# Edge stage of a four-layer graph network: four tiles summed in one cleared PSUM bank, one 512-column add on VectorE

## The chip, the cores and the metric

The kernel runs on one core of one Trainium2 chip, as one launch. The metric is the device time of a launch in microseconds: before the change three timed runs gave 4739.2, 4741.78 and 4747.91, median 4741.78 us. Beside them stands one profiled execution of the same kernel.

## The reference, cut to what matters

Four graph layers follow one another on 6250 nodes of 128 features; the edge list has 106250 entries (50000 drawn edges in both directions and a loop at every node), sorted by `dst`. Only the last layer is touched:

```
e_in     = concat([x[src], x[dst]])                    # per edge
edge_new = relu(e_in @ We1 + be1) @ We2 + be2
agg      = segment_sum(edge_new, dst, num_segments=N)
mesh_new = relu(concat([x, agg]) @ Wn1 + bn1) @ Wn2 + bn2
x        = layernorm(x + (x + mesh_new))
```

The first product splits in two node products, P = x·We1(upper) and Q = x·We1(lower) + be1, so an edge needs relu(P[src] + Q[dst]), and We2 can be applied after the sum over edges. The edge stage computes, for each node, the sum of relu(P[src] + Q[dst]) over its edges.

## The kernel before, in words

**Tiles.** Nodes lie in 49 blocks of 128. Edges are put in an order of the kernel's own and cut into 960 tiles of 128 edges, so that all edges of a tile have their `dst` in one block. Three sections follow one another: edges that need only the first 3 of 13 groups of P rows and have `dst` in blocks 0 to 29; the rest of those that need the first 6; and all others. In each the blocks rise. Within the setup stage VectorE works out each edge's sort value (lines 2569 to 2610), POOL scatters them to their places (line 1741), and VectorE writes the block number of every tile into the SBUF row `block_of` (lines 2700 to 2703).

**Spots.** The edge stage takes 8 tiles at a time: 120 spots, `Spot` in the code. The first 96 are 16 turns of six (`TURN = "DEDEDE"`); turn 0 and turn 15 are written out, turns 1 to 14 run in hardware loops; the last 24 are written out too. Of an "E" spot the rows P[src] were gathered earlier and come in by one DMA, of a "D" spot POOL gathers them now, eight indirect DMAs of 128 rows (line 1134). 48 spots are E, 72 are D, and the last 24 are all D.

**One spot**, on four engines that each run their own list in order:

- ACT turns the tile's `dst` values into a one-hot matrix with edges along the free side (lines 1206, 1208), then applies Relu to the two halves (line 1223).
- PE loads 8 block numbers from `block_of` into registers (`tile_blocks`, line 471; `snap`, line 472), multiplies the turned one-hots with Q of those blocks (line 1253, "q" below, fp32, 4 tiles in each of two banks), and then sums the spot before: one fp32 product per tile, relu'd rows times one-hot, 128 columns of its own in PSUM (line 1234, "sums" below). A second half of q waits for VectorE's first half of the spot before (semaphore `edge_pre`).
- VectorE makes the other one-hots for the next spot (line 1268, "hots"), loads the spot before's 8 block numbers, adds P rows and q of this spot in two halves of 512 columns (line 1284), and then adds the eight PSUM results of the spot before to `acc` at their blocks, one instruction of 128 columns per tile (line 1294), each waiting for the one ahead of it.
- SP issues the broadcasts of `dst` values and the E rows.

In PE's list q waits for `hot_ready`, which VectorE gives one spot earlier. In turns 0 to 12 PE also does half of a node product (lines 1240, 1241), which ACT copies (line 1218) before PE goes on.

Of the kernel before, what the change touches and what calls it, by code (L numbers as in the profile page):

```python
# [12 lines left out]
BF16 = mybir.dt.bfloat16  # L13
I32 = mybir.dt.int32
# [20 lines left out]
VB = NEAR_BLOCKS + 2 * NB  # L35
T = -(-((E + VB * (P - 1)) // P) // (2 * CH)) * 2 * CH
# [118 lines left out]
def gnn(nc, d):  # L155
    ctx = ExitStack()
    with ctx:
# [48 lines left out]
        ext_w = sb("ext_w", [P, EXT_BLOCKS])  # L206
        mv = sb("mv", [P, NBP, 2])
# [249 lines left out]
        hid_added = Count(S("added"), T)  # L457
# [9 lines left out]
        def tile_blocks(eng, c, which="block"):  # L467

            if (eng, which) not in block_regs:
                block_regs[eng, which] = [eng.alloc_register(f"{which}{u}") for u in range(CH)]  # L470
            eng.load(block_regs[eng, which], block_of[0:1, bass.ds(CH * c, CH)])  # L471
            return [eng.snap(r, min_val=0, max_val=NB - 1) for r in block_regs[eng, which]]  # L472
# [753 lines left out]
        def edge_pe(pe):  # L1226

            def sums_of(spot):
                h = spot.par
                for g, tiles in groups(P):  # L1230
                    wait(pe, S("added"), CH * (spot.u - 2) + tiles[-1] + 1)
                    wait(pe, S("edge_act"), 2 * spot.u + g + 1)
                    for u in tiles:
                        nc.tensor.matmul(psum_sum(h, u, P), ring_e[:, h * CH + u, :], hot_ring[spot.hot][:, u, :],  # L1234
                                         start=True, stop=True, skip_group_check=True).then_inc(S("summed"), 1)
# [7 lines left out]
            def body(spot):  # L1243
# [5 lines left out]
                wait(pe, S("hot_ready"), spot.u + 1)  # L1249
# [15 lines left out]
        def edge_dve(dve):  # L1265
# [8 lines left out]
            chain(dve)(nc.vector.tensor_copy(iota_bank, iota[:, :]))  # L1274
            hots(Spot(0, 0))
            chain(dve)(nc.vector.memset(acc[:, :], 0.0))
            last_of = {u: tiles[-1] for g, tiles in groups(P) for u in tiles}
# [10 lines left out]
            def adds_of(spot, blk):  # L1288
                for u in range(CH):
                    if u == 0 or last_of[u] != last_of[u - 1]:  # L1290
                        wait(dve, S("summed"), CH * spot.u + last_of[u] + 1)
                    dst = acc[:, bass.ds(blk[u] * P, P)]
                    wait(dve, S("added"), CH * spot.u + u)
                    nc.vector.tensor_tensor(dst, psum_sum(spot.par, u, P), dst, ALU.add).then_inc(S("added"), 1)  # L1294

            def body(spot):
                if not spot.last:
                    hots(spot.after())
                if not spot.first:
                    blk = tile_blocks(dve, spot.before().chunk)  # L1300
                gathered(spot)
                if not spot.first:
                    adds_of(spot.before(), blk)
                if spot.last:
                    adds_of(spot, tile_blocks(dve, spot.chunk))
# [1002 lines left out]
        def _(dve):  # L2308
# [261 lines left out]
            near_left, far_before, from_far = tiny[:, 10:11], first, edge_b[4][:, 0:EC]  # L2570
            step(nc.vector.tensor_scalar(behind_near, src_s, float(NEAR_TO), None, ALU.is_ge))
            step(nc.vector.scalar_tensor_tensor(behind_near, dst_s, float(NEAR_BLOCKS * P), behind_near, ALU.is_ge, ALU.max))
# [21 lines left out]
            step(nc.vector.scalar_tensor_tensor(key_i, behind_near, float(NEAR_BLOCKS * P), dst_s, ALU.mult, ALU.add))  # L2594
            step(nc.vector.scalar_tensor_tensor(key_i, far, float(NB * P), key_i, ALU.mult, ALU.add))
# [3 lines left out]
            step(nc.vector.tensor_copy(near_left, extra_ends[:, 0:1]))  # L2599
            counted_before(far_before, far)  # L2600
            step(nc.vector.scalar_tensor_tensor(prod, place, 2.0, ee, ALU.mult, ALU.subtract))
# [366 lines left out]
```

## Time and profile before

| what | value |
|---|---|
| median of three timed runs | 4741.78 us (4739.2 to 4747.91) |
| the profiled execution's span, first to last instruction | 7303.0 us |
| mean granted TensorE clock in it | 0.754 |
| busy over the span: PE, VectorE, ACT, POOL | 56%, 46%, 32%, 36% |
| edge stage in the profiled execution | about 6205 to 7255 us |

The profiled execution gives its span alone, no time of what lies around it, and this span is 2561 us longer than the timed median. It is therefore read for durations and order inside a stage, and not for shares of the timed run. The edge stage's own rows are to be read by spot: one line 1268 instruction on VectorE marks one spot.

### The profile page before, as it was taken

What the parts mean: (1) busy time and instruction counts of PE and PEld (TensorE: products, weight loads), DVE (VectorE), ACT (ScalarE), POOL (GpSimd) and SP (SyncE); (2) the same over time, 40 slices, a digit from 0 to 9 for tenths busy, and PEclk for the clock granted to TensorE, in tenths of its full rate; (3) what the DMA queues carried; (4) which work ended last, traced back from release to release, by engine and by line L of the source; (5) the groups of instructions that cost most, each with busy time, mean ns of one, the idle gap of its engine ahead of it and who ended that gap; (6) DMA issues with size and microseconds to landing.
All of it is one profiled execution on the core that took longest, in us unless ns stands there. A gap on an engine that the chain in (4) does not pass through costs nothing. (4 is left out here: it accounts for less than half of the span.)

```text
span 7303.0 us, 82736 instructions
## 1 busy us (share of the span) xinstructions
PE 4076.2 (56%) x24237; PEld 3354.5 (46%) x24238; DVE 3381.7 (46%) x7886; ACT 2340.3 (32%) x3120; POOL 2658.9 (36%) x2706
## 2 busy tenths in 40 slices
PE   4332641019981111117989798988672197666655
PEld 2111420007761101106778586858571197665644
DVE  4222540358970000106788776456451076555545
ACT  0000010005640000004555455557461075444433
POOL 4555157730017777770000000000427601444463
PEclk7665865559995555558999898989785598888777
DMA  9400000009970000116658287843444343444432
GB/s 376 155 0 0 0 2 0 0 23 334 368 250 0 0 0 0 28 25 222 232 189 293 96 293 214 296 162 95 132 125 124 97 139 98 132 132 130 130 95 67
DMA packets 364823, 923.20 MB, mean 126 GB/s; under 512 B 114026, under 2 KB 138716, under 8 KB 364531
## 3 DMA queue, kind: packets, MB, share of 16 engines
q1 hardware_dynamic: 214722, 650.09, 26.9%
q10 hardware_dynamic: 58609, 180.13, 6.4%
q0 software_dynamic: 91200, 89.42, 5.2%
q8 instruction: 142, 2.33, 0.1%
q14 instruction: 150, 1.23, 0.0%
HBM read 705.69 MB, written 213.71 MB: 126 GB/s over the span
## 5 line engine op out<-in xcount | busy, mean ns | idle before, releaser
L1741 POOL DMA_INDIRECT edges_halves<-local,gather_idx x832 | 854.9, 1027 | 791.7 <-SPq L372 505.4
L1680 POOL DMA_INDIRECT adj_t<-cell_val,cell_at x832 | 828.6, 996 | 465.2 <-issue 369.9
L862 PE MATMUL ps<-tiles_r,stage_r 128*128 128x512 f32 x2028 | 811.6, 400 | 158.2 <-issue 132.0
L1134 POOL DMA_INDIRECT big<-table,gather_idx x576 | 548.4, 952 | 832.3 <-DVE stage L1284 376.3
L869 PE MATMUL ps<-stage,big 128*128 128x130 f32 x4046 | 520.1, 284 | 370.3 <-issue 354.7
L1134 POOL DMA_INDIRECT x_fm<-table,gather_idx x384 | 370.2, 964 | 959.8 <-DMA table<-cell_at 689.7
L869 PEld LDWEIGHTS ps<-stage,big 128*128 128x128 f32 x4046 | 497.9, 199 | 388.5 <-issue 384.6
L2059 PE MATMUL ps<-big,ident_h 128*128 128x104 bf16 (+1 forms) x2880 | 359.7, 256 | 460.4 <-issue 459.7
L1253 PE MATMUL ps<-big,stage 128*128 x1920 | 356.2, 342 | 352.7 <-issue 189.3
L1319 PE MATMUL ps<-ident,big 128*128 128x128 f32 x260 | 73.3, 377 | 817.2 <-issue 768.2
L2442 DVE TENSOR_TENSOR big<-ps,stage 128x1248 bf16<-128x1248 f32 x192 | 270.7, 1451 | 519.5 <-remote 385.1
L755 ACT ACTIVATE big<-big,cols,stage 128x512 f32 (+1 forms) x508 | 371.7, 803 | 428.1 <-remote 273.9
L862 PEld LDWEIGHTS ps<-tiles_r,stage_r 128*128 128x128 f32 x2028 | 389.0, 192 | 257.3 <-issue 154.9
L2059 PEld LDWEIGHTS ps<-big,ident_h 128*128 128x128 bf16 x2880 | 233.9, 103 | 587.8 <-issue 515.3
L1253 PEld LDWEIGHTS ps<-big,stage 128*128 128x128 f32 x1920 | 307.2, 242 | 401.5 <-issue 401.2
L702 DVE TENSOR_SCALAR_CACHE_REDUCE big<-ps 128x512 f16<-128x512 f16 (+2 forms) x724 | 430.0, 651 | 131.4 <-remote 77.9
L797 ACT CAST tiles_r<-onehot 128x1024 fp32r<-128x1024 f16 x338 | 355.0, 1050 | 380.4 <-DMA onehot<-adj_t 127.1
L1746 POOL DMA_INDIRECT big<-edges_halves,pair_idx x8 | 7.7, 958 | 1196.5 <-DVEq L372 1194.4
L1319 PEld LDWEIGHTS ps<-ident,big 128*128 128x128 f32 x260 | 37.1, 181 | 854.7 <-issue 803.8
L864 PE MATMUL ps<-tiles_r,lower_r 128*128 128x512 f32 x1016 | 405.9, 400 | 0.0
L864 PE MATMUL ps<-tiles_r,lower_late 128*128 128x512 f32 x1012 | 398.8, 394 | 0.0
L2761 DVE SCALAR_TENSOR_TENSOR big<-ps,cols,big 128x256 f32<-128x256 f32 x78 | 37.4, 480 | 720.1 <-remote 658.3
(482 smaller groups left out, 9007.8 us busy)
## 6 DMA issues: line engine op xcount, KB each, us to landing
onehot<-adj_t SPq DMA_DIRECT2D x332, 512.0 KB
big<-adj_t SPq DMA_DIRECT2D x332, 512.0 KB
onehot<-adj_s SPq DMA_DIRECT2D x170, 512.0 KB
adj_t<-rows ACTq DMA_DIRECT2D x13, 6656.0 KB
adj_s<-big ACTq DMA_DIRECT2D x157, 512.0 KB, 5.3
stage<-local_rows SPq DMA_DIRECT2D x120, 512.0 KB
big<-adj_s SPq DMA_DIRECT2D x84, 512.0 KB
x_fm<-adj_s SPq DMA_DIRECT2D x84, 512.0 KB
```

What stands on the lines that cost most here:

```text
L702: last = nc.vector.tensor_scalar(turned[turn % RING][:, j, of, :].rearrange("p m c -> p (m c)"), flips[turn % 2][:, j, of, :].rearrange("p ...
L755: nc.scalar.activation(tile32[s][:, m * GW:(m + 1) * GW], r_rows[:, bass.ds(g * GW, GW)], ACT.Relu, bias=col(MINUS_ONE), scale=stage_nm[:, ...
L797: nc.scalar.copy(tile_r[s][:, 0:TW // 2], raw_tile(p, s)[:, 0:TW // 2]).then_inc(S("cast_act"), 1)
L862: nc.tensor.matmul(psum_fm(p, n)[:, 0:cut], upper_rows[:, k, :], tile[:, 0:cut], start=k == 0, stop=False, skip_group_check=True)
L864: last = nc.tensor.matmul(psum_fm(p, n)[:, 0:cut], lower_of(p)[:, k, :], tile[:, 0:cut], start=False, stop=k == NBP - 1, skip_group_check= ...
L869: last = nc.tensor.matmul(psum_nm(p, n, j), tile[:, j * P:(j + 1) * P], stage_nm[:, k, 0:AW], start=k == 0 and j % 2 == 0, stop=k == NBP - ...
L1134: return nc.gpsimd.indirect_dma_start(out, None, table[0:N, :], bass.IndirectOffsetOnAxis(gather_idx[:, t:t + 1], 0))
L1253: last = nc.tensor.matmul(spot.q_bank(g)[:, (u % 4) * P:(u % 4 + 1) * P], ring_ohT[:, h * CH + u, :], q_nm[:, bass.ds(blk[u] * P, P)], sta ...
L1680: nc.gpsimd.indirect_dma_start(out, bass.IndirectOffsetOnAxis(cells[:, c:c + 1], 0), cell_val[:, c:c + 1], None).then_inc(S(name), 16)
L1741: nc.gpsimd.indirect_dma_start(edges_halves, bass.IndirectOffsetOnAxis(slot_at[:, at:at + 1], 0), slot_val[:, at:at + 1], None).then_inc(h ...
L2059: return nc.tensor.matmul(ps[:, bank, of], stationary, moving, start=False, stop=True, skip_group_check=True)
L2442: nc.vector.tensor_tensor(eq[done % 4], own_keys(n).unsqueeze(1).to_broadcast([P, SHIFTS, SLW]), bass.AP(behind.tensor, behind.offset, [be ...
```

## The change

A window of four neighbouring tiles now has one cleared PSUM bank of 512 columns, which stands for four neighbouring blocks. PE clears it with a bf16 product of `ident_h` and a blank operand, and then adds each tile's product (`start=False`) at the 128 columns of its block within the window. VectorE adds the whole bank to `acc` in one 512-column instruction, so two adds for a spot in place of eight. For this the tiles' order must let any four neighbours span at most four blocks: the first section now takes blocks 19 to 48 rising, the middle one runs backward from 48 to 0, the last one rises again. Three tables replace the one: the block of a tile, its column within the window, the window's first block. PE loads a second set of 8 registers per spot, VectorE loads 2 in place of 8.

```diff
@@ sums_of (PE), lines 1228 on
-                for g, tiles in groups(P):
-                    wait(pe, S("added"), CH * (spot.u - 2) + tiles[-1] + 1)
+                column = tile_columns(pe, spot.chunk)
+                wait(pe, S("hot_ready"), spot.u + 1)
+                for g in range(2):
+                    wait(pe, S("added"), 2 * (spot.u - 2) + g + 1)
+                    nc.tensor.matmul(ps[:, 2 * h + g, :], ident_h[:, :], blank, start=True, stop=True,
+                                     skip_group_check=True)
                     wait(pe, S("edge_act"), 2 * spot.u + g + 1)
-                    for u in tiles:
-                        nc.tensor.matmul(psum_sum(h, u, P), ring_e[:, h * CH + u, :], hot_ring[spot.hot][:, u, :],
-                                         start=True, stop=True, skip_group_check=True).then_inc(S("summed"), 1)
+                    for u in range(WINDOW * g, WINDOW * (g + 1)):
+                        last = nc.tensor.matmul(ps[:, 2 * h + g, bass.ds(column[u] * P, P)], ring_e[:, h * CH + u, :],
+                                                hot_ring[spot.hot][:, u, :], start=False, stop=True, skip_group_check=True)
+                    last.then_inc(S("summed"), 1)
@@ body (PE): q no longer waits for the hots
                 wait(pe, S("hot_turned"), spot.u + 1)
-                wait(pe, S("hot_ready"), spot.u + 1)
@@ VectorE
-            def adds_of(spot, blk):
-                for u in range(CH):
...
-                    nc.vector.tensor_tensor(dst, psum_sum(spot.par, u, P), dst, ALU.add).then_inc(S("added"), 1)
+            def add_of(spot, g, window):
+                wait(dve, S("summed"), 2 * spot.u + g + 1)
+                wait(dve, S("added"), 2 * spot.u + g)
+                dst = acc[:, bass.ds(window[g] * P, WINDOW * P)]
+                nc.vector.tensor_tensor(dst, ps[:, 2 * spot.par + g, :], dst, ALU.add).then_inc(S("added"), 1)
             def body(spot):
+                if not spot.first:
+                    window = half_windows(dve, spot.before().chunk)
+                gathered(spot)
+                if not spot.first:
+                    add_of(spot.before(), 0, window)
                 if not spot.last:
                     hots(spot.after())
                 if not spot.first:
-                    blk = tile_blocks(dve, spot.before().chunk)
-                gathered(spot)
-                if not spot.first:
-                    adds_of(spot.before(), blk)
+                    add_of(spot.before(), 1, window)
@@ setup: sort value of an edge (832 columns each)
+            step(nc.vector.tensor_scalar(backward, dst_s, 7, 8, ALU.logical_shift_right, ALU.logical_shift_left))
+            step(nc.vector.tensor_tensor(middle, behind_near, far, ALU.subtract))
+            step(nc.vector.tensor_tensor(backward, backward, middle, ALU.mult))
...
@@ setup: tables, twice, 480 columns each; the four steps of 2700 to 2703 become ten
+                step(nc.vector.tensor_scalar(later_half, block, -2.0, float(NEAR_BLOCKS + NB - 1 - NEAR_FROM), ALU.mult, ALU.add))
...
+                step(nc.vector.tensor_reduce(windows, later_half.rearrange("p (w t) -> p w t", t=WINDOW), AX_X, ALU.min))
...
```

`tile_columns` and `half_windows` are `tile_blocks` with another table and with 8 and 2 values. The blank operand is `w_hh` read as bf16, set to zero once ahead of the stage.

## Rows read from the trace of the kernel before

**Rows 1.** The page: chain that ended last; two groups of indirect DMAs.

```profile
PE 13%; issue 10%; DVE 4%; DVEq 3%; another core or an unknown queue 2%; ACT 0%; DMA 0%; SPq 0%; ACTq 0%
...
L1741 POOL DMA_INDIRECT edges_halves<-local,gather_idx x832 | 854.9, 1027 | 791.7 <-SPq L372 505.4
...
L1134 POOL DMA_INDIRECT big<-table,gather_idx x576 | 548.4, 952 | 832.3 <-DVE stage L1284 376.3
```

**Rows 2.** Busy us (instructions) by engine, PEclk, DMA: looped part, last spots.

```profile
6250.00:6983.00 733.00, 496.04 (x2994) 446.57 (x2993) 430.75 (x1008) 319.57 (x379) 348.58 (x367) 0.82 0.42 130
6983.00:7255.00 272.00, 128.95 (x697) 114.97 (x695) 104.22 (x248) 72.31 (x86) 153.94 (x162) 0.68 0.28 77
```

**Rows 3.** Line 1268 in 6250 to 6980 us: count and ns min/median/max.

```profile
L1268 DVE TENSOR_TENSOR onehot<-ps,local x61: 1211/1212/1225, 6249.0 to 6971.6; 128x1024 f32<-128x1024 f32 x61
L1268 DVE TENSOR_TENSOR rows<-ps,local x31: 1211/1211/1225, 6256.0 to 6978.1; 128x1024 f32<-128x1024 f32 x31
```

**Rows 4.** Timeline of VectorE, one looped spot: start, duration, instruction, count, idle before it.

```profile
6509.02 1.21 DVE L1268 TENSOR_TENSOR onehot<-ps,local 128x1024 f32<-128x1024 f32 x1
6511.37 1.29 DVE L1284 TENSOR_TENSOR stage<-ps,big 128x512 f32<-128x512 f32 x2 [1.14 <-issue]
...
6514.38 1.59 DVE L1294 TENSOR_TENSOR acc<-ps,acc 128x128 f32 x4 [0.21 <-DVE acc L1294]
6515.89 1.21 DVE L1268 TENSOR_TENSOR onehot<-ps,local 128x1024 f32<-128x1024 f32 x1
```

**Rows 5.** Timeline of VectorE, one written-out spot.

```profile
6965.08 1.21 DVE L1268 TENSOR_TENSOR onehot<-ps,local 128x1024 f32<-128x1024 f32 x1
...
6971.60 1.21 DVE L1268 TENSOR_TENSOR onehot<-ps,local 128x1024 f32<-128x1024 f32 x1
```

**Rows 6.** Register loads by line, ns min/median/max: 8, 8 values, snap, 1 value.

```profile
L471 PEldq TENSOR_LOAD <-block_of x120: 1917/1922/1942, 6196.5 to 7235.5; - x120
L471 DVEq TENSOR_LOAD <-block_of x120: 686/1827/1850, 6211.2 to 7251.9; - x120
...
L472 PEldq FUSED_REGOPS  x120: 150/172/176, 6198.5 to 7237.4; - x120
...
L583 SPq TENSOR_LOAD <-need x13: 262/271/813, 1567.3 to 2092.5; - x13
```

**Rows 7.** Timeline of PE: a spot that waits for nobody, then a pause.

```profile
6546.02 2.05 PE L1253 MATMUL ps<-big,stage 128*128 x16 [0.47 <-issue]
6547.90 1.95 PE L1234 MATMUL ps<-onehot,stage 128*128 128x128 f32 x16
6550.36 1.93 PE L1253 MATMUL ps<-big,stage 128*128 x14 [0.51 <-issue]
6553.36 0.27 PE L1253 MATMUL ps<-big,stage 128*128 x1 [1.07 <-issue]
```

**Rows 8.** Timeline of PE: q at the lower clock; q that waited for hots.

```profile
6561.41 3.78 PE L1253 MATMUL ps<-big,stage 128*128 x16 [2.22 <-DVE onehot L1268]
...
6575.23 1.15 PE L1253 MATMUL ps<-big,stage 128*128 x8 [2.30 <-DVE rows L1268]
```

**Rows 9.** PE's address steps ahead of four q products, in 6569.8 to 6570.3 us.

```profile
L1253 PEldq FUSED_REGOPS  x4: 46/46/46, 6569.9 to 6570.3; - x4
```

**Rows 10.** Waits, 6250 to 6983: who, for whom, us, times, longest.

```profile
ACT x_fm L1218 <- remote: 60.2, 8, 9.2
```

**Rows 11.** Waits in 6983 to 7255 us.

```profile
DVE stage L1284 <- remote: 77.4, 11, 10.7
```

**Rows 12.** 512-column add; 416-column bf16 product. Columns as in rows 3.

```profile
L1284 DVE TENSOR_TENSOR stage<-ps,big x240: 678/691/693, 6209.5 to 7248.2; 128x512 f32<-128x512 f32 x120
...
L2055 PE MATMUL ps<-rows,ident_h x16: 339/526/534, 31.2 to 910.6; 128*128 128x416 bf16 x8, 128*128 128x392 bf16 x8
```

**Rows 13.** Setup steps on VectorE: a 480-column one and an 832-column one.

```profile
L2703 DVE TENSOR_TENSOR block_of<-big 128x480 int16<-128x480 f32 x2 | 1.3, 658 | 0.1
...
L2604 DVE SCALAR_TENSOR_TENSOR big<-big,acc x1: 1085/1085/1085, 984.4 to 984.4; 128x832 f32<-128x832 f32 x1
```

More of the change, by code:

```diff
@@ L206, in gnn @@
         ext_w = sb("ext_w", [P, EXT_BLOCKS])
+        block_row, column_row, window_row = block_of[0:32, :], block_of[32:64, :], block_of[64:96, 0:T // WINDOW]
+        blank = w_hh.bitcast(BF16)[:, 0:WINDOW * P]
         mv = sb("mv", [P, NBP, 2])
@@ L465, in gnn, with values_at, tile_blocks, tile_columns @@
         block_regs = {}
-        def tile_blocks(eng, c, which="block"):
+        def values_at(eng, which, table, per, c, most):
             if (eng, which) not in block_regs:
-                block_regs[eng, which] = [eng.alloc_register(f"{which}{u}") for u in range(CH)]
-            eng.load(block_regs[eng, which], block_of[0:1, bass.ds(CH * c, CH)])
-            return [eng.snap(r, min_val=0, max_val=NB - 1) for r in block_regs[eng, which]]
+                block_regs[eng, which] = [eng.alloc_register(f"{which}{u}") for u in range(per)]
+            eng.load(block_regs[eng, which], table[0:1, bass.ds(per * c, per)])
+            return [eng.snap(r, min_val=0, max_val=most) for r in block_regs[eng, which]]
+        def tile_blocks(eng, c):
+            return values_at(eng, "block", block_row, CH, c, NB - 1)
+        def tile_columns(eng, c):
+            return values_at(eng, "column", column_row, CH, c, WINDOW - 1)
+        def half_windows(eng, c):
+            return values_at(eng, "window", window_row, CH // WINDOW, c, NB - 1)
         def groups(w):
@@ L1274, in edge_dve @@
             chain(dve)(nc.vector.tensor_copy(iota_bank, iota[:, :]))
+            chain(dve)(nc.vector.memset(blank, 0.0))
             hots(Spot(0, 0))
             chain(dve)(nc.vector.memset(acc[:, :], 0.0))
-            last_of = {u: tiles[-1] for g, tiles in groups(P) for u in tiles}
             def gathered(spot):
@@ L2569, in _ @@
             behind_near, far, key_i = edge_a[0][:, 0:EC], col_v.bitcast(F32), ahead.bitcast(I32)
[L2570 removed]
+            far_before, from_far = first, edge_b[4][:, 0:EC]
+            middle, backward = edge_b[4][:, 0:EC], edge_b[5][:, 0:EC].bitcast(I32)
             step(nc.vector.tensor_scalar(behind_near, src_s, float(NEAR_TO), None, ALU.is_ge))
[L2572 removed]
+            step(nc.vector.scalar_tensor_tensor(behind_near, dst_s, float(NEAR_FROM * P), behind_near, ALU.is_lt, ALU.max))
             step(nc.vector.tensor_scalar(far, src_s, float(MIDDLE_TO), None, ALU.is_ge))
```

49 lines of the change are left out of this document (28 added, 21 removed).

## The prediction

> **What bounds the kernel now.** I read the page first. Its chain of waits attributes little of the span, and the profiled span is 7303.0 us where the timed median is 4741.78. The two differ by 2561 us. The page's groups show where that can lie: POOL's indirect DMAs, some 2640 of them, each busy 0.95 to 1.03 us [rows 1]; if nearly all of that were the profiler's, 2640 times 0.97 is 2561. That is an argument and not a measurement, but it says that a stage in which POOL is late in the profile need not be so in a timed run. So I take durations from the profile and add my sum to the timed median.
>
> Next, the edge stage by stretches. In the looped part, 733 us hold 61 + 31 = 92 spots [rows 2, 3], 7.97 us each, and no engine is full: PE 496 us, VectorE 431, ACT 320, POOL 349. The timeline shows the limit all the same. One undisturbed spot on VectorE runs from 6509.02 to 6515.89 us, 6.87 us, without a pause that another engine causes: hots 1.21, then 1.14 of "issue", the two 512-column adds 1.29, then eight block adds of which four take 1.59, with 0.21 between the fours [rows 4]. The 1.14 is VectorE's own register load: 8 values take 1.83 us [rows 6], it starts with the hots, and what is longer than they are is left over. So VectorE's own list sets the best spot. Written out, without counters to compute, a spot takes 6.52 us [rows 5]. The other 7.97 - 6.87 = 1.10 us per spot are disturbances: PE pauses such as 1.07 us ahead of a single product [rows 7], and ACT's wait of 60.2 us in all for the node product, eight times [rows 10].
>
> PE is second. When nobody held it up, one spot took 6550.36 - 6546.02 = 4.34 us, at the clock's upper level [rows 7]. Elsewhere q had to wait 2.2 to 2.3 us and started when the hots were there [rows 8]. POOL waits for VectorE in the stage, 376.3 us of it [rows 1]; only in the last 24 spots, all gathers, is it late in the profile: VectorE waits 77.4 us for "remote", which is the landing of rows [rows 11], and 272 us go into some 24 spots [rows 2].
>
> **The change, part by part.**
>
> *VectorE, per spot.* Eight adds go (1.59 + 0.21 + 1.59 = 3.39 us), two 512-column adds come; their price is that of the add of the same shape, 0.69 us each [rows 12]. The load falls from 8 values to 2 and now stands ahead of everything, beside the last add of the spot before. For 2 values there is no row; one value takes 0.27 us on SP, eight 1.83 [rows 6]. I take 0.5, close to the one-value row, and charge nothing: 0.69 us of add cover it. New list: 1.29 + 0.69 + 1.21 + 0.69 = 3.9, with semaphore steps 4.0 us in place of 6.87. If VectorE stayed the bound, 2.9 us per spot would be gained.
>
> *PE, per spot.* This is where I expect the price. PE's instruction list gets a second load of 8 values, 1.92 us, and its snap, 0.17 [rows 6], with address and start steps some 2.25 us. Can it hide? The first load does: it is issued when the sums are all queued, and q starts 0.51 us after the sums' end although the load is 1.92 long [rows 7]. But what stands behind a load isn't issued before it is done; VectorE's 1.14 us show it [rows 4]. The second load stands between q and the sums. It covers q's execution, the first covers the sums', but both stand in one list, and the list's length is then the spot. 4.34 us, which was mostly that list already (load 1.92, snap 0.17, address steps and waits), becomes 6.6.
>
> The eight sums now need an address step each, because their column is a register: q's four steps begin within 0.4 us, 0.13 apart [rows 9], so eight are 1.0 us at most, and nothing if they run beside what issuing a product takes anyway. I take the middle, 0.5. Two blanks and one more wait: a 416-column bf16 product takes 0.53 us at the low clock, 0.34 at best [rows 12]; where the list is the bound it is only the issue that counts. Bounds 0.15 and 1.1; I take 0.25, because PE's array has slack at the upper clock (4 of 7.4 us busy). PE's spot is then 4.34 + 2.25 + 0.5 + 0.25 = 7.35, call it 7.4 us; with all low ends 6.75, with all high ends 8.7.
>
> *What is late next.* PE's 7.4 is above VectorE's old 6.87. q no longer waits for the hots, which takes away the old link, but PE's own list takes its place. Behind PE's second load stand the sums, VectorE's adds of that spot and q of the next. ACT (two 1.1 us steps, two 0.6 us steps) and SP (broadcast, early rows) have slack of over 3 us. VectorE will have 3 us of idle time per spot. POOL's gathers are released by VectorE's 512-column adds, and come with them.
>
> *Sum.* 7.4 - 6.87 = 0.53 us per spot. I keep the disturbances at 1.10 us, so a looped spot goes from 7.97 to 8.50: 92 spots, +49 us. For the 28 written-out spots I take the same 0.53, 6.52 to 7.05: +15. In the profiled execution 24 of these hide behind POOL, so the profiled span grows less.
>
> *Setup.* The sort value costs two more 832-column steps, 1.09 us each [rows 13], less three one-column steps: +1.7. The tables cost ten steps in place of four, twice: twelve more at up to 0.66 us [rows 13], some on a quarter of the columns or on 32 rows, taken at 0.6: +7. They end the stage and the next begins behind them, so all of it is on the path: +9 in all (bounds 4 and 12). The blank's memset is below 0.3 us. The order of the edges changes which rows are gathered when, not how many; nothing counted.
>
> Total: +49 + 15 + 9 = +73, 4741.8 + 73 = 4815 us. For the profiled span: 0.53 times 96 plus 9, 7303 + 60 = 7363.
>
> **The rivals.**
>
> *VectorE's gain arrives (faster).* If PE's second load lay beside q as cheaply as the first lies beside the sums, PE's spot would be 4.34 + 0.5 + 0.25 = 5.1, above VectorE's 4.0: -1.77 us times 120, plus 9, gives 4741.8 - 203 = 4538 us. For it: VectorE bounds the best spots today, and half of its list goes. Against it: PE has 6.87 - 4.34 = 2.5 us to spare per spot and is asked for 3.0. The point from which it decides is PE's added list at 2.5 us. The Trainium skill's page VectorE: DVE Perf Modes, in its section on the TRN2 errata, says that operations on SBUF data pay a fixed cost per instruction, and advises tiles of 512 elements or more. By that rule alone this change pays, and it would come out near this rival; the trace agrees on the add itself (four of 128 columns 1.59 us, one of 512 0.69).
>
> *The disturbances are soaked up (slightly faster).* Today's 1.10 us are partly VectorE's own pauses and waits of VectorE for PE. A PE that runs 7.4 us at every spot, with VectorE idle 3, may show fewer. At 7.4 flat: 92 times -0.57, plus 15 and 9, is -28: 4714 us. Against it: the pauses and the node wait seen above are PE's, and PE will have no slack for them.
>
> *PE at the low clock (slower than forecast).* The granted clock is 0.82 in the looped part [rows 2], so PE is at 1.2 GHz for part of it; 16 q products then take 3.78 us where they took 2.05 [rows 7, 8]. At that level q, sums and two blanks are 3.41 + 3.41 + 1.06 = 7.9 us per spot (3.41 is 3.78 less the last product's own tail), and the array is the bound: 0.5 more per spot, +60, 4875 us. The new pause between q and sums speaks for it. The Trainium skill's page TensorE: Matmul & The Clock Gate, section on HAM oscillation, says that pauses between bursts of products bring the slow level back; a load between q and sums is such a pause.
>
> *It doesn't do what it says.* If lists on both engines end within 0.1 us of today's (the sums' address steps free and the blanks too: 4.34 + 2.25 + 0.15 = 6.74), the stage stays where it is and the setup's 9 us alone are left, partly paid back: 4745 us.
>
> **How the numbers follow.** Forecast 4815: 0.46. Low clock, 4875: 0.20. VectorE's gain, 4538: 0.14. Disturbances soaked up, 4714: 0.14. Nothing, 4745: 0.06. The likeliest case's own range, from PE's spot at 6.75 to 8.2 us (8.7 would need every high end at once), is 4736 to 4910. The range given, 4700 to 4890, leaves out the gain of VectorE and the end of the low-clock case, some 0.2. A change of under 0.2% (9.5 us) can't be told from none; faster by more: 0.14 + 0.13 = 0.27; within: 0.09 (the nothing case and the forecast's low edge); slower: 0.64.
>
> **What would show it.** Right: a spot of PE at 7.2 to 7.6 us with two register loads of 1.9 us in it; VectorE idle about 3 us per spot, waiting for PE's products; adds at 0.69; the looped part about 780 us. VectorE's step: its list at 4.0. Sums' address steps: their spacing against q's. Low clock: a granted clock under 0.75 there and products spaced 0.21. Setup: the table steps 12 more. Wrong: spots of 5 to 6 us, or a PE that issues products while a load is under way; then the list isn't the bound and the gain is real.

## The result, and the profile after

The kernel after takes 4803.31 us (median of four runs, 4796.83 to 4806.61) where the kernel before takes 4742.0 (four runs, 4739.2 to 4747.91): ratio 1.0122, 95% interval 1.0107 to 1.0137, so 51 to 65 us slower. The forecast was 4815, its range 4700 to 4890.

The profile of before that stands ahead is of an unusually long execution (span 7303.0 us). The kernel before was therefore profiled once more, as e0_before: 4750.88 us, span 4749.1. The span of after is 4795.1, of a run of 4796.83. From here on "before" in a trace means e0_before. Its span is within 2 us of its time, as after's is.

Two stretches of before, the first 96 spots and the 24 that only gather (columns as in [rows 2]):

```profile
3803.00:4463.00 660.00, 460.61 (x3076) 411.26 (x3076) 443.28 (x1028) 334.80 (x393) 364.19 (x383) 0.90 0.50 153
4463.00:4695.00 232.00, 143.87 (x808) 132.78 (x808) 118.42 (x278) 84.67 (x100) 167.41 (x176) 0.77 0.39 103
```

The same two of after:

```profile
3803.00:4518.00 715.00, 456.49 (x3204) 398.36 (x3252) 358.80 (x471) 334.95 (x396) 363.21 (x382) 0.97 0.44 140
4518.00:4746.00 228.00, 138.65 (x862) 121.08 (x873) 93.68 (x126) 82.95 (x98) 166.54 (x176) 0.86 0.36 102
```

The loss is all in the first stretch. VectorE has 84 us less to do there and PE's array no more than before, at a granted clock of 0.97 against 0.90, and the stretch still takes 55 us longer: by busy time no engine is full. What to read then is not an engine's busy time but its list of instructions. One plain spot of after, on PE (start, duration, instruction, idle before it):

```profile
4037.52 2.05 PE L1270 MATMUL ps<-big,stage 128*128 x16 [1.32 <-ACT stage L1221]
4041.16 1.15 PE L1251 MATMUL ps<-onehot,stage 128*128 128x128 f32 x8 [1.60 <-ACT stage L1236]
...
4044.85 0.37 PE L1270 MATMUL ps<-big,stage 128*128 x1 [1.43 <-issue]
```

```profile
L475 PEldq TENSOR_LOAD <-block_of x2: 1917/1918/1918, 4038.7 to 4042.4; - x2
...
L476 PEldq FUSED_REGOPS  x2: 150/162/173, 4040.6 to 4044.4; - x2
...
L1251 PEldq FUSED_REGOPS  x8: 46/50/60, 4041.1 to 4042.2; - x8
```

The spot is 4044.85 - 4037.52 = 7.33 us, and the list fills it: from q's start 1.2 us until the column load is issued, 2.5 until the sums start (load 1.92, snap, start steps), 1.2 until the block load, 2.4 until the next q. The array pauses 1.60 and 1.43 us, once behind each load. The profile names ACT as releaser of one of them. The load's end (4038.7 + 1.92 = 4040.6) and its snap stand right ahead of the sums, and the list goes on from there without a stop: the pause is the load's. Of [rows 7] the first half is unchanged, a load of 1.92 behind the sums; the second is new.

VectorE in the same spot:

```profile
4036.99 0.68 DVE L1309 TENSOR_TENSOR acc<-ps,acc 128x512 f32 x1
4038.81 1.48 DVE L1301 TENSOR_TENSOR stage<-ps,big 128x512 f32<-128x512 f32 x2 [1.15 <-PE ps L1270]
4042.46 0.69 DVE L1309 TENSOR_TENSOR acc<-ps,acc 128x512 f32 x1 [2.16 <-PE ps L1251]
4043.06 1.22 DVE L1285 TENSOR_TENSOR rows<-ps,local 128x1024 f32<-128x1024 f32 x1
```

(The adds answer to [rows 12].) It waits 1.15 + 2.16 = 3.3 us for PE. Its list is 7.2 - 3.3 = 3.9 us (hots to hots, 4035.86 to 4043.06), and the new add takes 0.69. In before the same spot has VectorE's own pace, as in [rows 4]:

```profile
4101.10 1.22 DVE L1268 TENSOR_TENSOR onehot<-ps,local 128x1024 f32<-128x1024 f32 x1 [0.26 <-issue]
4103.59 1.29 DVE L1284 TENSOR_TENSOR stage<-ps,big 128x512 f32<-128x512 f32 x2 [1.27 <-issue]
...
4108.11 1.21 DVE L1268 TENSOR_TENSOR rows<-ps,local 128x1024 f32<-128x1024 f32 x1
```

By the starts of VectorE's hots a looped turn of six spots takes 41.8 us before (7.22 7.00 6.91 6.86 6.96 6.85) and 45.9 after (9.35 7.37 7.32 7.38 7.27 7.24). Five spots lose 0.4 us each, and the first of the turn loses 2.1. Ahead of it stand the half of a node product and the end of the hardware loop's turn. PE after, with the node product (lines 1258, 1259) between sums and q:

```profile
4020.83 2.05 PE L1270 MATMUL ps<-big,stage 128*128 x16 [1.35 <-issue]
4024.46 1.15 PE L1251 MATMUL ps<-onehot,stage 128*128 128x128 f32 x8 [1.59 <-issue]
...
4026.55 1.02 PE L1258 MATMUL ps<-x_fm,w_late 128*128 x2
4027.51 1.12 PE L1259 MATMUL ps<-cell_at,row 1*128 1x512 f32 x2
4029.87 3.03 PE L1270 MATMUL ps<-big,stage 128*128 x16 [1.24 <-ACT x_fm L1231]
```

and PE before:

```profile
4133.01 1.95 PE L1234 MATMUL ps<-onehot,stage 128*128 128x128 f32 x16
...
4138.20 2.80 PE L1253 MATMUL ps<-big,stage 128*128 x16 [1.33 <-ACT x_fm L1218]
```

Both have the same pieces and end in a wait for ACT's copy, from the sums' start to q's 5.2 us before and 5.4 after. From q to q this spot is 9.04 us after (4020.83 to 4029.87) and the next 7.65 (to 4037.52). Before, PE had 2.5 us to spare per spot and all of it lay beside VectorE's list; after, PE has none.

The 2.1 us are two things. The last loops (turns 13 and 14) have no node product. Where turn 13 ends, the same two spots are still 7.91 and 7.94 us:

```profile
4434.78 2.05 PE L1270 MATMUL ps<-big,stage 128*128 x16 [1.35 <-issue]
...
4442.69 2.86 PE L1270 MATMUL ps<-big,stage 128*128 x16 [1.96 <-issue]
...
4450.63 1.95 PE L1270 MATMUL ps<-big,stage 128*128 x16
```

By VectorE's hots that turn takes 44.8 us where the others take 45.9. So about 1.1 us are the wait for the node product's copy, and about 1.0 is left to the loop's end: its branch and counter steps stand in PE's list too, with some 0.5 us; where the other half lies is open (one branch, in 4024 to 4031 us):

```profile
L1131 PEldq COMPARE_BRANCH  x1: 207/207/207, 4025.9 to 4025.9; - x1
```

Before, a turn takes 41.8 us with the node product and without it.

**Where the 46 us between the two profiled executions are** (start of the first gathered add, of the 193rd and of the last, line 1284 or 1301): setup and earlier layers 3814.4 to 3808.8 (-5.6), 96 spots 662.5 to 720.1 (+57.6), the gathering spots 217.3 to 216.4 (-0.9), from the last such add to the end 54.9 to 49.9 (-5.0). The first is scatter (3807.3 to 3821.2 in the kernels below). The last comes back in every kernel with the two large adds (49.5 to 49.9 against 54.5 to 55.1 in those with eight): eight adds no longer stand behind the last sums.

### The profile page after: what moved, and what is told of

Its sections match the earlier page's. It is cut to its first block and busy times, and to the rows that moved or that the text cites. A ratio compares the mean times of both kernels' runs of the same rounds, so it can differ in the third digit from the quotient of the medians.

```text
span 4795.1 us, 82164 instructions
## 1 busy us (share of the span) xinstructions
PE 3822.2 (80%) x24417; PEld 3183.1 (66%) x24478; DVE 3304.8 (69%) x7179; ACT 2336.5 (49%) x3120; POOL 2670.3 (56%) x2706
## 5 line engine op out<-in xcount | busy, mean ns | idle before, releaser
L882 PE MATMUL ps<-stage,big 128*128 128x130 f32 x4046 | 466.6, 277 | 18.8 <-DVE big L1036 15.8
L882 PEld LDWEIGHTS ps<-stage,big 128*128 128x128 f32 x4046 | 461.3, 193 | 19.5 <-issue 12.4
L1270 PE MATMUL ps<-big,stage 128*128 x1920 | 267.3, 295 | 174.7 <-issue 110.5
L1270 PEld LDWEIGHTS ps<-big,stage 128*128 128x128 f32 x1920 | 242.3, 204 | 206.6 <-issue 206.5
L1301 DVE TENSOR_TENSOR stage<-ps,big 128x512 f32<-128x512 f32 x240 | 166.0, 692 | 277.9 <-PE ps L1270 159.4
L1236 ACT ACTIVATE stage<-stage 128x512 f32<-128x512 f32 x240 | 148.4, 627 | 390.2 <-DVE stage L1301 389.8
L2078 PE MATMUL ps<-big,ident_h 128*128 128x104 bf16 (+1 forms) x2880 | 318.1, 247 | 9.1 <-issue 8.7
L1046 DVE CAST tiles_r<-onehot 128x1024 fp32r<-128x1024 f16 x338 | 246.9, 731 | 107.8 <-PE ps L877 91.3
L1309 DVE TENSOR_TENSOR acc<-ps,acc 128x512 f32 x240 | 164.7, 686 | 213.7 <-PE ps L1251 213.3
L875 PE MATMUL ps<-rows_r,stage_r 128*128 128x512 f32 x676 | 269.6, 399 | 39.5 <-ACT rows_r L810 36.1
```

The source lines that it names most:

```text
L875: nc.tensor.matmul(psum_fm(p, n)[:, 0:cut], upper_rows[:, k, :], tile[:, 0:cut], start=k == 0, stop=False, skip_group_check=True)
L882: last = nc.tensor.matmul(psum_nm(p, n, j), tile[:, j * P:(j + 1) * P], stage_nm[:, k, 0:AW], start=k == 0 and j % 2 == 0, stop=k == NBP - ...
L1046: nc.vector.tensor_copy(tile_r[s][:, TW // 2:TW], raw_tile(p, s)[:, TW // 2:TW]).then_inc(S("cast_dve"), 1)
L1270: last = nc.tensor.matmul(spot.q_bank(g)[:, (u % 4) * P:(u % 4 + 1) * P], ring_ohT[:, h * CH + u, :], q_nm[:, bass.ds(blk[u] * P, P)], sta ...
L2078: return nc.tensor.matmul(ps[:, bank, of], stationary, moving, start=False, stop=True, skip_group_check=True)
```

## The experiments

**e1_static: the kernel after without its column load.** Each tile's product goes to column u mod 4 of its bank. Left out: the sums lie at the wrong blocks.

```diff
-                column = tile_columns(pe, spot.chunk)
-  ... ps[:, 2 * h + g, bass.ds(column[u] * P, P)] ...
+  ... ps[:, 2 * h + g, u % WINDOW * P:(u % WINDOW + 1) * P] ...
```

> The changed kernel without the column registers: tile u of a window is always summed at column u mod 4, so sums land at wrong blocks; no second load on PE, no address step for the sums, all else as it is. Theory (PE's list is the bound and the load with its address steps is its new part): PE's list falls by 2.4 + 0.6 us from 7.3 to about 4.3; then POOL's gathers (8 times 1.26 us for every two spots, 5.0 us a spot) or chains of waits are next: looped spots of 5.0 to 5.6 us, 4590 to 4650 us. Rival (the blanks, the array's clock or the accumulating form are the cost): 4790 to 4810 us, no change.

Measured: 4575.45 us, ratio to before 0.9645 (0.9628 to 0.9661), below the forecast of 4590 to 4650. Turns of 29.7 to 31.3 us; plain spots 4.43 to 4.50 where after has 7.3. With the load and the address steps gone the change would be worth 3.5%: these two are what it paid with. More could hardly come out, whatever PE's list does: POOL's gathers now follow one another almost without a stop. In 3900 to 4250 us there are 277, with 4.7 us in all in which POOL waits for VectorE. That is 1.26 us for each, 30.3 for the 24 of a turn, and the turns average 30.4.

**e2_once: the columns loaded once, ahead of the stage.** All spots use the first chunk's columns (again wrong blocks).

```diff
+            column = tile_columns(pe, 0)
             def sums_of(spot):
-                column = tile_columns(pe, spot.chunk)
```

> The changed kernel with the eight columns loaded once, ahead of the stage, in place of once per spot: sums land at wrong blocks; the address steps of the sums stay, the load per spot goes. Theory: the load with snap and start steps is 2.4 us of PE's list, so the list is 4.9 us; looped spots 5.1 to 5.8 us, 4600 to 4660 us, at most 20 us above the kernel with static columns. Rival (the address steps of the sums are most of the price): within 20 us of 4803.

Measured: 4578.89 us, 0.9648 (0.9632 to 0.9664), below its forecast too, with the same spots. It was to keep the address steps and take out the load alone. It didn't: with columns that never change the addresses were worked out once. Line 1251's address steps, first e2_once, then after, over the whole run:

```profile
L1251 PEldq FUSED_REGOPS  x16: 46/46/60, 3823.2 to 3829.4; - x16
```

```profile
L1251 PEldq FUSED_REGOPS  x960: 46/55/60, 3813.0 to 4747.0; - x192
```

So e1 and e2 are one experiment, and neither splits load from address steps. That the address steps are free doesn't follow. What follows is that at least 7.33 - 4.45 = 2.88 us hang on both. One spot of e2_once, PE, and the block loads:

```profile
4111.95 2.05 PE L1270 MATMUL ps<-big,stage 128*128 x16 [0.18 <-issue]
...
4116.43 0.82 PE L1270 MATMUL ps<-big,stage 128*128 x5 [0.23 <-issue]
```

```profile
L475 PEldq TENSOR_LOAD <-block_of x2: 1922/1924/1927, 4109.5 to 4114.0; - x2
```

q, blanks (the clearing products) and sums now follow one another with 0.2 us between them and one load beside them, 4.48 us in all. Here the list is no longer what is full. The load starts 4114.0 - 4111.95 = 2.05 us after q, though only waits and the sums' issue stand behind q's address steps; in after a load stood 1.2 us behind q's start. The list is held up there, as it seems behind the array's products, so what left it is probably more than 2.88 us.

**e4_load: the kernel before with a second, unused load of 8 values on PE.**

```diff
             def sums_of(spot):
+                tile_blocks(pe, spot.chunk, "idle")
```

> The kernel before with one part of the change alone: PE loads 8 more values per spot between q and the sums, and uses none. Theory (PE's list runs beside VectorE's, and only the longer counts): PE's list goes from 4.3 to 6.6 us, just under VectorE's 6.9, so the best spots stay and the disturbances grow: 4745 to 4790 us. Rival (a load on PE is always on the path, in full): 2.2 us times 96 spots, 4950 us. Rival (a load costs nothing): 4742.

Measured: 4748.11 us, 0.9999 (0.9988 to 1.0009). It tells nothing but how well a null is measured: no instruction used the registers and the load was dropped in the build; the trace has 121 loads on PE, as before's.

**e4b_load_used: the same, and used.** Two of eight sums take their column from a loaded value shifted to 0; the output is unchanged.

```diff
+                pe.load(block_regs[pe, "idle"], block_of[0:1, bass.ds(CH * spot.chunk, CH)])
+                idle = [pe.snap(r, min_val=0, max_val=127) for r in block_regs[pe, "idle"]]
...
+                        at = (idle[u] >> 6) * P
```

> The kernel before with one part of the change alone: PE loads 8 more values per spot between q and the sums; two of them enter (shifted to zero) into the address of two sums, so that the load is kept. Theory (a spot takes the longer of the two lists): PE's list goes from 4.34 to about 6.95 us (load, snap and start 2.45, two address steps), VectorE's stays at 6.97: spots of 6.9 to 7.3 us, 4742 to 4780 us. Rival (a load on PE is always on the path): 2.45 us times 96 spots, about 4980 us. Rival (free): 4742 to 4746 us.

Measured: 4747.97 us, 0.9999 (0.9989 to 1.0008), turns 41.8 to 42.4 for the most part. The load is there, and so are its pauses:

```profile
L1232 PEldq TENSOR_LOAD <-block_of x2: 1919/1920/1920, 4101.4 to 4108.0; - x2
```

```profile
4100.40 2.05 PE L1258 MATMUL ps<-big,stage 128*128 x16 [1.00 <-issue]
4103.92 2.04 PE L1239 MATMUL ps<-onehot,stage 128*128 128x128 f32 x16 [1.47 <-issue]
4106.98 2.05 PE L1258 MATMUL ps<-big,stage 128*128 x16 [1.02 <-DVE stage L1289]
```

This pair of q's stands 6.58 us apart, so PE can do a spot in that with the load in it. My 4.34 + 2.25 is 6.59, which agrees better than it should, as said further down. Both are below VectorE's 6.9, which stays the pace, so the load costs nothing here. The same load costs in after, where VectorE's list is 3.9. It is the crossing of two lists, not the load by itself, that sets the price.

**e6_no_blank: after without the two clearing products** (the banks keep adding up, so the sums are not the reference's).

```diff
-                    nc.tensor.matmul(ps[:, 2 * h + g, :], ident_h[:, :], blank, start=True, stop=True,
-                                     skip_group_check=True)
```

> The changed kernel without the two blank products per spot: banks are never cleared, so the sums are wrong; all else as it is. Theory: in PE's list the blanks cost what issuing them takes, 0.1 us each; 7.3 to 7.1 us a spot, 4780 to 4795 us. Rival (their 512 columns run on the path, 0.21 us each at the upper clock, 0.43 at the lower): 4740 to 4765 us.

Measured: 4802.73 us, 1.0107 (1.009 to 1.0124); turns 45.5 to 45.6 for the most part against 45.9. The blanks cost 0.06 us a spot. They are 0.38 us of array each, beside a list that is late anyway. The forecast of 4780 to 4795 had them cost more.

**e3_two_values: the column worked out from the block.** PE keeps the block registers of q and loads only the two window values (2 in place of 8); column = block - window. Nothing is left out.

```diff
-                column = tile_columns(pe, spot.chunk)
+                window = values_at(pe, "window", window_row, CH // WINDOW, spot.chunk, NB - 1)
+                kept = [pe.snap(r, min_val=0, max_val=NB - 1) for r in block_regs[pe, f"block{h}"]]
+                column = [(kept[u] - window[u // WINDOW]) ... for u in range(CH)]
...
-                blk = tile_blocks(pe, spot.chunk)
+                blk = values_at(pe, f"block{h}", block_row, CH, spot.chunk, NB - 1)
```

> The changed kernel with a shorter second load on PE: the 2 window starts in place of the 8 columns, and the column worked out in registers as the tile's block (kept from q's load of the spot before) less its window's start. Theory (the price of a load is its number of values): load 0.5 to 0.7 in place of 1.92 us, one snap of 8 kept values more, perhaps one step more per sum: PE's list 5.9 to 6.4 us in place of 7.3, 4660 to 4715 us, faster than both kernels. Rival (a load has a high fixed price whatever its length): 4770 to 4800 us.

Measured: 4721.85 us, 0.9941 (0.9925 to 0.9958), turns 40.4, plain spots 6.4: faster than both kernels, though above the forecast of 4660 to 4715. The two loads of one spot, 0.695 us for 2 values and 2.104 for 8, the eight address steps with a subtraction in each, and PE's spot of 6.40 us:

```profile
L475 PEldq TENSOR_LOAD <-block_of x2: 695/1400/2104, 4201.9 to 4204.6; - x2
...
L1253 PEldq FUSED_REGOPS  x8: 69/69/75, 4203.1 to 4204.3; - x8
```

```profile
4200.77 2.05 PE L1272 MATMUL ps<-big,stage 128*128 x16 [1.65 <-ACT stage L1221]
...
4207.17 2.05 PE L1272 MATMUL ps<-big,stage 128*128 x16 [1.65 <-ACT stage L1221]
```

Six values fewer take 1.23 us off the column load, and the spot gets 0.93 shorter; 0.18 went back into the other load, the rest into address steps, 0.15 apart in place of 0.13. The load here is part of the path one for one.

**e8_packed: one load for both numbers.** PE loads 8 values that hold block and column, once a spot, for q; the sums use the same registers a spot later. The setup's formula put other numbers in them than meant, so blocks and columns are not the graph's; the instructions are the same as in e8b.

```diff
-                column = tile_columns(pe, spot.chunk)
+                packed = [pe.snap(r, ...) for r in block_regs[pe, f"packed{h}"]]
+                column = [v & (WINDOW - 1) for v in packed]
...
+                blk = [v >> 2 for v in values_at(pe, f"packed{h}", block_row, CH, spot.chunk, WINDOW * NB - 1)]
```

> The changed kernel with no second load on PE: one table holds 4 times the block plus the column, PE loads 8 values per spot as before the change and takes the block with a shift for q and the column with a mask for the next spot's sums. Theory: PE's list is 7.3 - 2.45 + 0.2 (snap of kept values) + up to 0.1 for each of 16 shifts and masks, 5.1 to 6.6 us; with the gathers' 5.03 us a spot behind it, 4590 to 4700 us; the setup changes by less than 2 us. If shifts and masks go into the address steps that are there, it is the faster of this and the two-value kernel by 50 us or more. Rival (the accumulating sums or the order of the list are the price): 4790 to 4805 us.

Measured: 4693.01 us, 0.9883 (0.9866 to 0.9899).

**e8b_packed: the same with 4 * block + column in the registers.**

```diff
+                step(nc.vector.tensor_scalar(later_half[0:32, :], later_half[0:32, :], float(WINDOW + 1), None, ALU.mult))
+                step(... block_row[:, half] = that less the window ...)
```

> The kernel after with one value per tile, 4 times its block plus its column (computed in the setup as 5 times the block less the window). TensorE loads these 8 values once, for q, shifts them right by 2 for the block, and takes the low 2 bits of the same registers for the sums a spot later; no second load stands ahead of the sums. Nothing is left out. In e8_packed the same instructions ran on values built by another formula, so that blocks and columns were not the graph's; here they are. Theory (TensorE's list is the spot, and its second load is what the change paid with): spots of 6.1 to 6.4 us in place of 7.66, a ratio of 0.985 to 0.991, 4680 to 4710 us. Rival (the wrong addresses of e8_packed made it quick, by touching few blocks): near e3_two_values or above, 4720 to 4760 us.

Measured: 4694.99 us (4692.56 to 4705.02), 0.991 (0.9896 to 0.9923), turns 38.7 for the most part, the others up to 40.8. Nothing is left out. This is the fastest such version: by the medians 47 us under before (4742.09 in these runs) and 108 under after. One spot, registers and PE:

```profile
L475 PEldq TENSOR_LOAD <-block_of x2: 1921/1922/1922, 4205.2 to 4211.5; - x2
...
L1252 PEldq ALU_OP  x8: 32/32/36, 4203.0 to 4204.8; - x8
L1252 PEldq FUSED_REGOPS  x8: 46/55/60, 4203.1 to 4204.9; - x8
```

```profile
4201.37 2.05 PE L1271 MATMUL ps<-big,stage 128*128 x16 [0.55 <-issue]
...
4207.63 2.05 PE L1271 MATMUL ps<-big,stage 128*128 x16 [2.00 <-ACT stage L1221]
```

With one load left the spot is 6.26 us, not 4.45. The mask and the address are two instructions per product, and eight pairs take 4203.0 to 4204.9 = 1.9 us, where the eight address steps of after took 4041.1 to 4042.2 = 1.1. So register arithmetic in the list counts as loads do. The list again makes up the spot: sums' part 4203.0 to 4205.2, load to q's first step 2.3, and q's part with a shift in each of its address steps the 1.8 that are left.

**e5_hots: after with q's wait for the hots put back.**

```diff
                 wait(pe, S("hot_turned"), spot.u + 1)
+                wait(pe, S("hot_ready"), spot.u + 1)
```

> The kernel after with one line more: TensorE's wait for VectorE's hots stands ahead of the q products again, as in the kernel before (the wait that was added ahead of the sums stays). Nothing is left out. Theory (TensorE's own list of instructions is the spot, VectorE is idle 3 us of it): the hots are there in time either way or all but, so 0 to +0.1 us per spot, ratio to before 1.011 to 1.016, 4798 to 4818 us. Rival (the moved wait is what keeps the change from being still slower, q overlaps the hots): q starts 0.5 to 1.2 us later in each spot, 4850 to 4940 us.

Measured: 4817.24 us (4814.72 to 4818.67), 1.0159 (1.0145 to 1.0172), turns 46.6. The profile now names the hots as q's releaser, but q starts hardly later, 7.37 us after the last:

```profile
4206.61 2.05 PE L1271 MATMUL ps<-big,stage 128*128 x16 [1.56 <-DVE onehot L1286]
...
4213.98 2.05 PE L1271 MATMUL ps<-big,stage 128*128 x16 [1.48 <-DVE onehot L1286]
```

0.12 us a spot, 14 us in all. The price is just above the theory's +0 to +0.1, and the time lies in its range. Whether it is the added step in the list or hots that end just then is not separated. That q could overlap the hots was worth little.

**e12_ahead: after with the column load right behind the block load,** ahead of the node wait and of q.

```diff
             def body(spot):
                 blk = tile_blocks(pe, spot.chunk)
+                column = None if spot.first else tile_columns(pe, spot.before().chunk)
```

> The kernel after with TensorE's load of the 8 columns moved from between q and the sums to the start of the spot, right behind the load of the 8 blocks and ahead of the wait for the node product. Nothing is left out. Theory (the list's length counts, not where in it a load stands, but where the list waits for something else a load placed ahead of that wait is covered): the five plain spots of a turn stay at 7.3 us, and the spot that waits for the node product falls from 9.35 to 7.3 to 8.4, so -10 to -27 us, 4775 to 4795 us, ratio to before 1.006 to 1.010. Rival A (the place counts: the load between q and sums covers q's execution, two loads in a row cover nothing): q starts up to 1.9 us later, spots of 8 us and more, 4850 us or above. Rival B (nothing moves): 4798 to 4808 us.

Measured: 4814.29 us (4810.99 to 4816.35), 1.0153 (1.0139 to 1.0167): 11 us slower than after where I forecast 10 to 27 faster. Neither rival fits either; by VectorE's hots spots alternate, mostly 5.8 to 6.8 and 8.8 to 9.6, turns 45.3 to 47.6. The loads in 4187 to 4196 us, and PE's q of six spots:

```profile
L475 PEldq TENSOR_LOAD <-block_of x3: 1922/1923/1926, 4187.5 to 4195.7; - x3
```

```profile
4184.86 2.05 PE L1272 MATMUL ps<-big,stage 128*128 x16 [1.68 <-issue]
...
4192.23 3.51 PE L1272 MATMUL ps<-big,stage 128*128 x16 [3.11 <-issue]
...
4200.48 2.05 PE L1272 MATMUL ps<-big,stage 128*128 x16 [2.52 <-issue]
...
4207.73 2.66 PE L1272 MATMUL ps<-big,stage 128*128 x16 [2.99 <-issue]
...
4215.04 2.05 PE L1272 MATMUL ps<-big,stage 128*128 x16 [1.42 <-issue]
...
4223.05 3.24 PE L1272 MATMUL ps<-big,stage 128*128 x14 [1.83 <-ACT x_fm L1231]
```

The pauses that after has twice a spot, 1.6 and 1.4, are mostly one of 2.5 to 3.1 here. Behind the one of 3.11 us q comes at the lower clock (16 products in 3.51 us against 2.05), behind that of 2.52 it doesn't. Over 585 us of looped spots the granted clock is 0.89, against 0.98 in after (first e12_ahead, then after):

```profile
3850.00:4435.00 585.00, 404.32 (x2620) 363.58 (x2619) 286.56 (x378) 267.47 (x318) 286.76 (x302) 0.89 0.43 138
```

```profile
3850.00:4435.00 585.00, 371.65 (x2613) 321.50 (x2650) 291.67 (x383) 268.94 (x319) 292.41 (x308) 0.98 0.43 139
```

PE's own rows say where the 11 us are. Counted from q to q, the plain spots whose q ran at the upper clock (2.05 us) average 7.33 us in this stretch, as in after (7.32): 26 spots, two loads in a row and all, like 4184.86 to 4192.23. The 14 whose q took 3.2 us or more average 8.28, like 4192.23 to 4200.48; the rest lie between. And the gain hoped for at the node wait is there: 4215.04 to 4223.05 is such a spot, 8.01 us in place of 9.04, and so are 9 of 12; the other three have a slowed q and take 9.1. So the theory's two halves hold, and low-clock spots that it had not reckoned with take back more than it gains. In after's order a slow q costs nothing: three spots there have one (3.2 us or more) and take 7.66 us, the same as their like at the upper clock. There a load lies beside q and another beside the sums; here both loads come when q and sums have been issued, so that slow products are on the path (the likeliest reading, not tested by itself). VectorE's hots, which alternate, hide all this. It has to be read on the engine that sets the pace.

**e11_setup: before with twelve more 480-column steps in the setup's tables.**

```diff
             for j ... :
+                for _ in range(6):
+                    step(nc.vector.tensor_scalar(far_half, block, NEAR_BLOCKS - 0.5, float(NEAR_BLOCKS), ALU.is_ge, ALU.mult))
```

> The kernel before with twelve steps more of 480 columns on VectorE where the setup makes its tables of blocks (each writes a tile that is written again before it is read). Nothing is left out. My forecast's term: the table steps end the setup and all that follows is behind them, so the first load of the next stage and the end of the kernel both come 8 us later, 4756 us, ratio 1.0017. Theory formed since (the next stage's start is set by GpSimd's scatters, which start at the same time in the kernels before and after, so the steps are hidden): the first load of the next stage comes 8 us later, the scatters' start at 1227 us and the end move by less than 2 us, ratio 0.9992 to 1.0006.

Measured: 4744.9 us (11 runs, 4736.48 to 4754.83), 1.0008 (0.9999 to 1.0017). In the trace the next stage's first load moves by 8.8 us and the scatters behind it don't: the scatters of line 1741 start from 1227.5 to 2326.8 us before and from 1226.8 to 2326.7 in e11_setup. The loads, before and then e11_setup (the two times in a row are first and last start):

```profile
L577 SPq DMA_DIRECT2D onehot<-adj_t x91: 327/328/434, 687.0 to 1201.1; - x91
```

```profile
L577 SPq DMA_DIRECT2D onehot<-adj_t x91: 327/328/433, 695.8 to 1201.5; - x91
```

In after the loads are from 694.6 to 1201.3 and the scatters from 1226.9 to 2327.5. The first load is 7.6 or 8.8 us late, the last one 0.2 or 0.4: the delay is gone by then. What paces the stretch is probably POOL (not shown by an experiment), whose scatters into `adj_t`, some 436, run from 600.2 to 1167.3 us in before, and to 1168.3 and 1167.3 in the others. The profiled end is 1.7 us earlier than before's. The timed ratio lies above the theory's span and its interval just reaches the rival's 1.0017, so by the times alone 0 to 8 us remain possible; by the trace it is nothing.

## Why the prediction was right, and where it was not

**PE's list as the new bound: right.** Forecast 7.2 to 7.6 us for PE's spot with two loads of 1.9 in it, VectorE idle 3 us, its list 4.0, the add 0.69. Measured 7.33, 1.918 twice, 3.3, 3.9, 0.69. e3, e8b and e1 each take something out of that list and the spot follows. e6 takes out array work and e5 puts a wait back, and it moves by 0.06 and 0.12. e4b has such a load under VectorE's longer list, and it is free.

**Its terms.** Load, snap and starts 2.25: the trace has 2.19 from the load's issue to the list's next step, by PE's pauses 2.4 to 2.5. Blanks 0.25: 0.06 (e6). Address steps 0.5: 0.69 by what 7.33 - 4.45 leaves, and 1.1 by their own rows in after (eight from 4041.1 to 4042.2), which is the high end that I had given. The base of 4.34 was too high in turn. I had called it mostly list, but as in e2_once part of it is the array: without that, 7.33 less 2.2 and 1.1 leaves about 4.0 (an estimate from these rows). Errors of 0.2 to 0.6 us of either sign met in a sum of 7.35, so that its nearness to 7.33 is in part luck. The mechanism is not.

**The gain of 0.53 per looped spot: mis-sized.** 7.40 - 6.87 was the difference of two undisturbed spots, and the plain spots gave 0.40 (five plain spots of a turn average 7.32 and 6.92). But the average over a turn is 7.66 - 6.97 = 0.69. The missing piece is the end of a turn, 2.1 us: about 1.1 for the node product's wait and about 1.0 for the steps with which the loop turns. The wait I had read [rows 10] and put in the 1.10 us of disturbances that stay; the loop's steps in PE's list I had at nothing. Before, both were covered by PE's 2.5 us of slack, and I had said myself that PE would have none for the wait. 2.1 us in each of the 14 looped turns are 29 of the 58 us, about half of them the node wait (13 times) and half the loop's end. e12_ahead, which puts a load ahead of that wait, gets 1.04 us of it back.

**The disturbances of 1.10 us a spot: absent.** They belonged to the one long execution. Undisturbed, before's looped spot is 6.97 and not 7.97. As the term stood on both sides it did no harm to the sum.

**The reading of 2561 us as the profiler's: wrong.** In e0_before POOL's indirect DMAs last the same 0.95 to 0.97 us and the span equals the time within 2 us. They are real time. The long execution lost its time elsewhere, most of it before this stage: its first gathered add starts at 6209.5 us, e0_before's at 3814.4.

**The written-out spots, +15: wrong, by that same reading.** Only those of turns 0 and 15 can lose. In turn 15 and the spots behind it they go from 6.52 to 6.8, some 3 us over 12. The last spots are POOL's in the timed run too. In after, eight DMAs per spot:

```profile
L1147 POOL DMA_INDIRECT big<-table,gather_idx x165: 947/952/961, 4534.5 to 4740.5; - x165
```

206.0 / 164 = 1.256 us per DMA, 10.05 a spot in both kernels, whatever PE's list does.

**The setup, +9: size right, place wrong.** 7.6 us later at the next stage's first load, and none 500 us on (e11). I had taken "the next begins behind them" for "all of it is on the path".

**What the sum comes to.** Forecast +49 + 15 + 9 = 73. Measured by the trace, without the scatter ahead of the stage: +57.6 - 0.9 - 5.0 = 52; by the medians 61 (interval 51 to 65). The -5.0 at the end I had not considered. 15 and 9 were for places that gave nothing, and the looped stretch was 9 short: the total is nearer than its parts, and that is luck.

**The rivals.** VectorE's gain (4538): it didn't come, but e1 and e2 show what it would have been worth, 4575 to 4579, if the load and the addresses cost nothing. Disturbances soaked up (4714): there were none. Low clock (4875): the granted clock rose, 0.90 to 0.97 over the 96 spots, so PE was nearly always at the upper level, 2.4 GHz. The rule of the Trainium skill that I cited for it (TensorE: Matmul & The Clock Gate, HAM oscillation: pauses between bursts bring the slow level back) isn't borne out by after's pauses of 1.2 to 1.6 us. In e12_ahead it is in part: behind a pause of 3.11 us q ran at the lower level, behind one of 2.52 at the upper, and 0.89 was granted.

## What to carry to other kernels

When an engine's work is cut and another's list gets longer, add up the second list, instruction by instruction, with register loads and address arithmetic in it. Its array may be idle and the list still be the bound. Whatever its slack covered until then, a wait or the end of a loop's turn, comes back at its full price. A load of registers costs by the value here (0.2 us each): pack two small numbers in one value (e8b_packed), or work the second out from the first (e3_two_values), before you load a second row. A profiled execution whose span is far from the timed median must be taken again before any of its stalls is priced; and a delay at the head of a stage is worth nothing if another queue paces that stage to its end.

## What the runs showed of the hardware that I had not expected

- Loads of registers from SBUF on PE: 8 values 1.92 us, 2 values 0.695; on VectorE 8 values 1.83, 2 values 0.507; (1.92 - 0.695) / 6 = 0.20 us per value on PE, 0.22 on VectorE. In e3_two_values the 8-value load took 2.09 to 2.10 on the same row, 0.17 longer; why is open.
- Address steps of a product come 0.12 to 0.14 us apart in the list, 0.15 with a subtraction, 0.23 with a mask as a separate instruction, although their own records show 0.03 to 0.07. Two bf16 products of 512 columns, 0.38 us each on the array, cost 0.06 us a spot there (e6_no_blank).
- Address steps from registers that never change, and loads that nobody uses, aren't there in the program that runs (16 steps in place of 960 in e2_once, 121 loads as before in e4_load). An experiment that means to keep them must be read in its trace first.
